# A two-layer recurrent block: layer-1 norm sums kept chunk by chunk in fp32, squared ReLU on ScalarE, the gate through tanh, and the Wq and Wk loads spread out

## The reference, cut to what matters

```
x: (8, 2048, 1024) fp32, one batch element for each core
# layer 0
xn = layernorm(x)
z = sigmoid(xn Wz^T + bz);  h~ = xn Wh^T + bh
s = scan over time of h_t = (1 - z + 1e-8) h_(t-1) + z h~
g = silu( (silu(xn Wg^T) * (xn Wu^T)) Wd^T )      # 3072 hidden, int weights / 127
x = x + s * g
# layer 1
xn = layernorm(x)
s = softmax((xn Wq^T / 32)(xn Wk^T)^T)(xn Wv^T)
xp = xn one token earlier (0 at the first)
xr = mu_r xn + (1 - mu_r) xp;   xk = mu_k xn + (1 - mu_k) xp
k = square(relu(xk W_k^T))
g = silu( sigmoid(xr W_r^T) * (k W_v^T) )
x = x + s * g
```

## Time and profile before

| | us |
|---|---|
| median of three runs | 1475.0 |
| lowest and highest | 1265.99, 1498.23 |
| profiled execution, device time | 1265.23 |
| its span (slowest core, 4) | 1264.2 |
| spans of the eight cores | 1260.6 to 1264.2 |
| TensorE busy | 1191.4 (94%) |
| VectorE busy | 592.3 (47%) |
| ScalarE busy | 299.5 (24%) |
| TensorE idle before its matmuls of L147 | 33.6 |

### The profile page before, as it was taken

The page is one execution under the profiler, slowest core; times in us unless marked ns, Lnnn a source line. Parts: engine busy times, 40 slices in busy tenths (PEclk is TensorE's granted clock), DMA queues, the critical chain, the costliest instruction groups (busy, mean ns, idle before and its releaser), DMA issues.

```text
span 1264.2 us, 16472 instructions; the slowest of 8 cores (1260.6 to 1264.2 us)
## 1 busy us (share of the span) xinstructions
PE 1191.4 (94%) x5728; PEld 547.4 (43%) x5728; DVE 592.3 (47%) x833; ACT 299.5 (24%) x398; POOL 123.4 (10%) x220
## 2 busy tenths in 40 slices
PE   1899999999999999999999786999999999999988
PEld 1344444444444444444444332444444444444443
DVE  3344121444446377144446488233134456556555
ACT  2333211233234211123234412333110101101110
POOL 1011111110111111111104012110000000000000
PEclk9899999999999999999999898999999999999999
DMA  9754844545454485355529647452000012123233
GB/s 202 200 89 85 194 81 71 100 101 112 100 106 67 67 195 93 65 115 104 110 54 151 116 84 131 86 101 83 1 1 1 1 43 80 52 78 83 84 84 117
DMA packets 56963, 116.52 MB, mean 92 GB/s; under 512 B 6704, under 2 KB 14896, under 8 KB 56880
## 3 DMA queue, kind: packets, MB, share of 16 engines
q0 software_dynamic: 31104, 65.03, 31.5%
q1 hardware_dynamic: 25776, 50.43, 12.9%
HBM read 159.47 MB, written 20.97 MB: 143 GB/s over the span
## 4 chain that ended last, share of the span: by engine, by line
PE 87%; DVE 8%; ACT 2%; issue 2%; DMA 1%; DVEq 0%; SPq 0%; ACTq 0%
PE PS L147 85%; DVE S L151 3%; PE PS L712 1%; DVE S L467 1%; DMA S<-xtok 1%; DVE S L426 1%; DVE S L465 1%; PE PS L259 1%; DVE S L463 1%; DVE S L246 1%; ACT S L265 0%; DVEq L62 0%; DVE CB L696 0%; ACT S L395 0%; ACT S L554 0%
## 5 line engine op out<-in xcount | busy, mean ns | idle before, releaser
L147 PE MATMUL PS<-S 128*128 128x512 bf16 x5248 | 1156.1, 383 | 33.6 <-DVE S L151 13.9
L147 PEld LDWEIGHTS PS<-S 128*128 128x128 bf16 x5248 | 514.6, 99 | 659.8 <-issue 61.1
L151 DVE TENSOR_TENSOR S<-S,PS 128x512 bf16<-128x512 bf16 (+1 forms) x128 | 88.0, 688 | 236.2 <-PE PS L147 171.8
L151 DVE TENSOR_TENSOR S<-S 128x512 f32<-128x512 f32 (+4 forms) x124 | 98.6, 795 | 46.7 <-ACT S L554 31.5
L299 ACT ACTIVATE S<-PS 128x512 bf16<-128x512 f32 x96 | 57.3, 597 | 223.7 <-PE PS L147 217.0
L700 ACT ACTIVATE S<-PS,CB 128x2048 bf16<-128x2048 f32 x16 | 31.5, 1967 | 247.9 <-DVE CB L698 247.9
L351 DVE TENSOR_SCALAR S<-S 128x512 f32<-128x512 f32 x32 | 13.7, 427 | 146.7 <-ACT S L346 146.7
L696 DVE TENSOR_REDUCE CB<-PS 128x1 f32<-128x1024 f32 x32 | 39.2, 1225 | 49.2 <-PE PS L739 31.0
L124 POOL DMA_DIRECT2D S<-wg x48 | 27.1, 565 | 307.0 <-PE PS L147 281.0
L638 DVE CAST S<-PS 128x512 bf16<-128x512 f32 x32 | 22.1, 691 | 55.4 <-PE PS L147 55.1
L151 DVE TENSOR_TENSOR S<-PS,S 128x512 f32<-128x512 f32 x32 | 22.1, 691 | 45.5 <-PE PS L147 45.5
(11 more groups left out here) (63 smaller groups left out, 484.1 us busy)
## 6 DMA issues: line engine op xcount, KB each, us to landing
S<-wg POOLq DMA_DIRECT2D x48, 256.0 KB, 4.1
S<-wu POOLq DMA_DIRECT2D x48, 256.0 KB, 4.7
S<-wd POOLq DMA_DIRECT2D x16, 768.0 KB, 7.4
S<-xtok SPq DMA_DIRECT2D x16, 512.0 KB, 17.9
S<-xt SPq DMA_DIRECT2D x16, 512.0 KB, 16.5
x1s<-S SPq DMA_DIRECT2D x16, 512.0 KB, 2.6
S<-x1s SPq DMA_DIRECT2D x32, 256.0 KB, 3.7
out<-S SPq DMA_DIRECT2D x32, 256.0 KB, 2.4
```

Source lines behind the costliest of these rows:

```text
L147: ins = te.matmul(dst, l, r, start=(i == 0), stop=(i == n - 1))
L151: return DVE.did(ve.tensor_mul(o, a, b))
```

## The change

Four things are changed.

- **Norm sums.** While `down_mix` runs chunk e, the new `stat_chunk(h, e - 1)` squares the previous chunk on ScalarE and adds it and its square to two fp32 accumulators on VectorE. After chunk 6 the two accumulators are split into a high and a low bf16 part. `ln1_steps` casts and squares only chunk 7, and sums over the partitions with 3 + 3 matmuls for each span instead of 8 + 8. It now has 17 steps: empty, `cast`, `sums` (both spans), `stat` (both spans), four `affine`, `edge`, eight with two `mix`.
- **Squared ReLU.** ReLU and Square both run on ScalarE, through an fp32 tile; VectorE has no part in it.
- **Gate.** Sigmoid becomes tanh of half the argument, VectorE computes (tanh + 1) * V in one instruction, and ScalarE writes silu of half of that straight into the output tile. That is one VectorE instruction less for each span.
- **Loads.** After each k-stage chunk o of half 0, one Wq piece and one Wk piece are issued, behind that chunk's weight load.

```diff
+        def stat_chunk(h, e):
+            accx, accq, sq = fp(ACCX, 1024), fp(ACCQ, 1024), fp(SQ, 1024)
+            xe = fp(X1 + e * 2048, 1024)
+            ACT.after(x1_tok[h, e], sq_free[0])
+            if e == 0:
+                DVE.after()
+                ACT.after((DVE.sem, DVE.sem.n))
+                acc_tok[h] = ACT.did(se.activation(accq, xe, AF.Square))
+                return
+            t = ACT.did(se.activation(sq, xe, AF.Square))
+            DVE.after()
+            DVE.did(ve.tensor_add(accx, fp(X1, 1024) if e == 1 else accx, xe))
+            DVE.after(t, acc_tok[h])
+            sq_free[0] = acc_tok[h] = DVE.did(ve.tensor_add(accq, accq, sq))
+            if e < 6:
+                return
+            for i, a in enumerate((accx, accq)):
+                DVE.after(mix_free[0])
+                t = DVE.did(ve.tensor_copy(bf(HILO[2 * i], 1024), a))
+                DVE.after(t)
+                acc_tok[h] = DVE.did(ve.tensor_sub(bf(HILO[2 * i + 1], 1024), a, bf(HILO[2 * i], 1024)))
 # down_mix, between the gate's silu and the z and h~ products
+            if e:
+                stat_chunk(h, e - 1)
 # ln1_steps
+            def cast():
+                xe = fp(X1 + 7 * 2048, 1024)
+                DVE.after(x1_tok[h, 7], acc_tok[h])
+                st["xb"] = DVE.did(ve.tensor_copy(xb, xe))
+                ACT.after(x1_tok[h, 7], sq_free[0])
+                st["sq"] = ACT.did(se.activation(sq, xe, AF.Square))
+            def sums():
+                for s in range(2):
+                    ...
+                    PE.after(acc_tok[h], st["xb"])
+                    st["mx", s] = (b, mms(ps(b), [(ones[:], r) for r in (hl[0], hl[1], xb[:, c])]))
+                    PE.after(st["sq"])
+                    st["mq", s] = (b, mms(ps(b), [(ones[:], r) for r in (hl[2], hl[3], sq[:, c])]))
+            steps = [lambda: None, cast, sums, stat]
+            for s in range(2):
+                for q in range(2):
+                    steps.append(lambda q=q, s=s: affine(q, s))
 # before the k stage
-        for c in range(NC8):
-            dma(POOL, bf(WQ + c * 1024, 1024), wqn[c], f_sem)
-            fold_tok = dma(POOL, bf(WK + c * 1024, 1024), wkn[c], f_sem)
 # k stage
-                    ACT.after(mm, rk_free[s], *t_free)
+                    ACT.after(mm, rk_free[s])
                     at = ACT.did(se.activation(rt, ps(b), AF.Relu))
                     bank_free[b] = at
-                    DVE.after(at)
-                    rk_free[s] = kact_tok[s] = mul(bf(KACT + o * 1024 + s * 512, 512), rt, rt)
+                    ACT.after(at)
+                    rk_free[s] = kact_tok[s] = ACT.did(se.activation(dst, rt, AF.Square))
                 w_done(k, mm)
                 if h == 0:
+                    dma(POOL, bf(WQ + o * 1024, 1024), wqn[o], f_sem)
+                    fold_tok = dma(POOL, bf(WK + o * 1024, 1024), wkn[o], f_sem)
                     step(late1)
 # gate stage
-                    ACT.after(mm, r_free[s], *rk_free)
-                    rtok.append(ACT.did(se.activation(bf(RS + s * 512, 512), ps(b), AF.Sigmoid)))
+                    ACT.after(mm, r_free[s])
+                    rtok.append(ACT.did(se.activation(fp(RS + s * 1024, 512), ps(b), AF.Tanh, scale=0.5)))
-                    t = mul(tv, bf(RS + s * 512, 512), ps(bk[s]))
+                    t = DVE.did(ve.scalar_tensor_tensor(tv, fp(RS + s * 1024, 512), 1.0, ps(bk[s]), ALU.add, ALU.mult))
-                    at = ACT.did(se.activation(sg, tv, AF.Sigmoid))
-                    DVE.after(at, go_tok[gq])
-                    t_free[s] = mul(gv, tv, sg)
+                    ACT.after(tt[s], go_tok[gq])
+                    t_free[s] = ACT.did(se.activation(gv, fp(TS + s * 1024, 512), AF.Silu, scale=0.5))
```

More of the change, by code:

```diff
@@ L33 @@
 ST = ZZ + 10240
-MD = ST + 2048
-COLS = MD + 1024
+SQ = ST + 2048
+COLS = SQ + 2048
 KACT, WQ, WK = HB, HB + 8192, HB + 16384
@@ L41 @@
 GG = HS + 2048
+MD, ACCX, ACCQ = ST, HS, ST
 AQK = ZZ
@@ L118, in sems @@
         return [sem(f"{name}{i}") for i in range(n)]
+    DGB = DG[:, 0:8]
     PE, DVE, ACT = Line(te, sem("s_pe")), Line(ve, sem("s_dve"), True), Line(se, sem("s_act"), True)
@@ L321, in x_load @@
             x_tok[h, e] = dma(SYN, fp(X1 + e * 2048, 1024), xt[e * 128:(e + 1) * 128, h * HT:(h + 1) * HT], x1_sem[e])
+        acc_tok = {}
+        sq_free = [None]
+        HILO = [TMP + i * 1024 for i in range(4)]
+        def stat_chunk(h, e):
[19 more added lines that the diff above has]
+                acc_tok[h] = DVE.did(ve.tensor_sub(bf(HILO[2 * i + 1], 1024), a, bf(HILO[2 * i], 1024)))
         def down_mix(h, e, kd, k):
@@ L375, in down_mix @@
             return mm
-        mub, rstd = fp(ST, 512), fp(ST + 1024, 512)
         xn1_tok = {}
@@ L383, in ln1_steps @@
             XR, XK = XRH[h], XKH[h]
-            steps = []
             st = {}
[L386 to L400, removed]
-                    PE.after(st["sq"])
[L402 to L408, removed]
@@ new lines, in ln1_steps @@
+            xb, sq = bf(SQ, 1024), bf(SQ + 1024, 1024)
+            stats = [(fp(ST, 512), fp(ST + 1024, 512)), (fp(SQ, 512), fp(SQ + 1024, 512))]
+            def cast():
[6 more added lines that the diff above has]
+                for s in range(2):
+                    c = slice(s * 512, (s + 1) * 512)
+                    hl = [bf(o, 1024)[:, c] for o in HILO]
+                    PE.after(acc_tok[h], st["xb"])
+                    b = bank()
+                    st["mx", s] = (b, mms(ps(b), [(ones[:], r) for r in (hl[0], hl[1], xb[:, c])]))
+                    PE.after(st["sq"])
+                    b = bank()
+                    st["mq", s] = (b, mms(ps(b), [(ones[:], r) for r in (hl[2], hl[3], sq[:, c])]))
@@ L409, in stat @@
+            def stat():
+                tok = [None, None]
+                for s in range(2):
+                    mub, rstd = stats[s]
+                    (bx, mx), (bq, mq) = st["mx", s], st["mq", s]
+                    DVE.after(mx, st["mq", 1][1])
+                    t = DVE.did(ve.tensor_scalar(mub, ps(bx), 1.0 / D, None, ALU.mult))
+                    bank_free[bx] = t
                     DVE.after(t)
                     t = mul(rstd, mub, mub)
-                    DVE.after(t, st["mq"])
@@ L412, in stat @@
[L412 to L430, removed]
@@ L432, in ln1_steps @@
-                steps += [cast, lambda: None, sums, stat, lambda: affine(0), lambda: affine(1)]
-                steps[-2] = lambda affine=affine: affine(0)
-                steps[-1] = lambda affine=affine: affine(1)
+                    DVE.after(t, mq)
+                    tok[s] = DVE.did(ve.scalar_tensor_tensor(rstd, ps(bq), 1.0 / D, rstd, ALU.mult, ALU.subtract))
+                    bank_free[bq] = tok[s]
+                for f, kw in ((AF.Ln, dict(bias=CB[:, EPS:EPS + 1])), (AF.Exp, dict(scale=-0.5))):
+                    for s in range(2):
+                        ACT.after(tok[s])
+                        tok[s] = ACT.did(se.activation(stats[s][1], stats[s][1], f, **kw))
@@ new lines, in stat, with affine @@
+                st["rstd"] = tok
+            def affine(q, s):
+                mub, rstd = stats[s]
+                xq = chunks(fp(X1 + q * 8192, 4096), 4)[:, :, s * 512:(s + 1) * 512]
+                tq = chunks(fp(TMP + q * 4096, 2048), 4)
+                mb = bass.broadcast_tensor_aps(xq, mub.rearrange("p (c j) -> p c j", c=1))[1]
+                rb = bass.broadcast_tensor_aps(xq, rstd.rearrange("p (c j) -> p c j", c=1))[1]
+                dst = chunks(bf(XN + h * 8192 + q * 4096, 4096), 4)[:, :, s * 512:(s + 1) * 512]
+                DVE.after(st["mq", 1][1])
+                t = DVE.did(ve.tensor_sub(tq, xq, mb))
+                DVE.after(t, st["rstd"][s], xn_ready)
+                xn1_tok[h, s] = mul(dst, tq, rb)
@@ L448, in edge @@
                     pv = chunks(bf(XN, 8192), 8)[:, :, 1023:1024]
-                    df = chunks(bf(MD + 1016, 8), 8)
+                    df = chunks(DGB, 8)
                     t = DVE.did(ve.tensor_sub(df, xf, pv))
@@ L461, in mix @@
                 df = S[:, MD:MD + hi - lo]
-                DVE.after(xn1_tok[h, part], st.get("md"))
+                DVE.after(xn1_tok[h, 1], st.get("md"))
                 t = DVE.did(ve.tensor_sub(df, x, p))
@@ L519, in build_program @@
             late1 = ln1_steps(h, pe_tok)
+            hs_free = collections.deque([acc_tok[h]] * 4)
             l0_tok = pe_tok
@@ L524, in build_program @@
         wvt_sem = sem("s_wvt")
-        kt_slot = collections.deque(range(2))
-        RS, TS, SG, GO = GG, HS, GG + 1024, ZZ
+        RS, TS, GO = GG, HS, ZZ
         r_free = [None] * 2
@@ L532, in build_program @@
         kact_tok = {}
-        rk_free = [None, None]
-        sg_free = None
+        rk_free = [acc_tok[1]] * 2
         ng = 0
@@ L583, in build_program @@
                 for s in range(2):
-                    tv = fp(HS + s * 1024, 512)
-                    DVE.after(rtok[s], vm[s], t_free[s])
```

(4 more changed lines are left out.)

6 lines of the change are left out of this document (2 added, 4 removed).

## The result

The changed kernel took 1228.4 us (four runs, 1228.3 to 1228.5), against 1264.9 to 1266.0 for the runs of the kernel before that belong with its profiled execution. The ratio is 0.9711, with a 95% interval of 0.9694 to 0.9728: 36.8 us less. (The higher times of the kernel before are executions in which the cores of a die ran at a lower clock; they are left out of every ratio here.) The forecast was 1222, 6 us too low, and inside its own range.

A forecast was written before the change was run, and what follows sets the result against it. Bound: TensorE's waits in layer 1 of half 0, behind VectorE's queue, ScalarE and late loads. That layer falls from 213 to 174.5 us, saving 38.5, plus 4.3 in layer 0: 1265.23 becomes 1222 us, range 1213 to 1238.

The forecast's parts named there:

- What bounds the kernel: Outside start-up, TensorE's idle time lies in one stage: layer 1 of half 0, where half 1's norm is stepped through.
- Norm sums, TensorE in layer 0: Half 0's 20 fewer sum matmuls, from a stretch TensorE fills, save 20 x 0.216 = 4.3 us.
- The prediction's own sign of being wrong: Wrong if TensorE waits in layer 0, or VectorE's last `mix` in half 0's gate stage ends after TensorE's last product there.
- the ring: k stage: banks (eight tiles, 13.8 us) cover ScalarE's and VectorE's lateness, but not at the stage's end.
- The k stage: ScalarE ends 3.3 us behind TensorE; V of span 1 waits 1.8 us for the last square in place of 10.84.
- Gate stage: Layer 1, half 0: VectorE's V passes free banks late for chunks 5 and 6, 2.5 us; half 1's k-stage wait goes.
- Tables: Gate stage: no table loads taken for tanh and silu; even alternating, 5.2 us a chunk stays under 6.91.
- Loads: First `wv` landing at 702.9 was a second hold on V's start; spread, loads cost nothing, by 2 to 3 us.
- Clock: Lower granted clock after one of the two waits in layer 1 of half 0: 1.7 us.
- The stage of before: Layer 1 in the kernel before: 213 us, from 662 to 875; afterwards 174.5.
- Rivals: VectorE keeps gate stage 1236 (0.15); late V or tables 1233 to 1236 (0.09); slow transfers 1252, no gain 1255 (0.09 together).
- the chain in `down_mix`: Layer 0: in-order square, addition and z passes hold TensorE; 5 us a chunk gives 1302 us; chance 0.05.

The follow-up runs named there:

- merged step: Changed kernel with sums and stat of the norm in one step, an empty step behind; 1228.3 and 1228.4 us.

## Why the prediction was right or wrong

- **What bounds the kernel.** Right. One stage held the waits, and 34.4 of the 36.9 us came from it.
- **Norm sums, TensorE in layer 0.** The step that failed: 4.3 us forecast with nothing against it, 2.0 measured. The prediction's own sign of being wrong, a wait of TensorE in layer 0, came in. The matmuls went, but the new `sums` takes four banks of eight in one step and `stat` releases them one step later, so TensorE, one hidden chunk of four banks on, finds the ring full: 1.88 us. (The other 0.3 had been lost ahead of the first sums.) I counted the instructions of the step and not the banks that it holds, though the prediction names the ring in the k stage. There VectorE is free and the banks come back in time; in layer 0 its list had the next hidden chunk's products first. The merged step shows it.
- **The k stage.** The mechanism was right, and the chain of ScalarE's work came out as laid down: 2.25 us for 1.8. The bound by VectorE's queue is shown with 14.3 us. The rule of the Trainium skill by which such work belongs on VectorE (ScalarE: Activation LUTs, Rules for kernel authors) fails in this place: with the square on VectorE the kernel takes 1245.3 us in place of 1228.4. The rule compares the two engines' speed for an element; here the queue that the square joins decides, with 14.3 us of wait for it and 2.6 for the cast behind it.
- **Gate stage.** Right in kind, small in size: 2.5 us forecast, 0.87 + 3.10 measured. VectorE's V passes ended 1.3 to 2.0 us later than laid down, counted from the k stage's start (662.0 there; 670.22 - 48 x 0.216 = 659.9 here). The first waited 1.51 us for tanh, which had a table load of 1.28 in front. My "no loads" forgot the one load behind Ln and Exp. No run takes that load away, so its share is not shown. The rounds before were read as 11.5 us; the two between 747.66 and 771.02 are 23.36, 11.7 each.
- **Tables.** Right. One load for 32 pairs of tanh and silu. The estimate by the figures of the Trainium skill (ScalarE: Activation LUTs, What ACT_TABLE_LOAD costs), 7.8 us a chunk, would have needed two changes of table in every chunk.
- **Loads.** Right that the queue was a second hold (11.7 us without the spreading). The bound of 10 us for a landing was too low (14.4), with no wait from it.
- **Clock.** Right, 1.7 us in the sum: the granted clock was 0.69 and 0.81 in the 7 us behind the 3.10 us wait, 0.31 x 3 + 0.19 x 4 = 1.7 us. That it came so close is partly luck, as a wait of 3.11 us had left no mark before.
- **The stage of before, misread.** I took 875 us as its end, the edge of a stretch. The last activation on R starts at 873.1. That made the saving 1.8 us too large. With 2.3 in layer 0 and 2.1 of waits (2.25 + 0.87 + 3.10 + 0.22 for 4.3) these are 6.2 us; the forecast was 6.0 too low, as the stretch behind gave back 0.5. (The start of half 1's k stage was forecast for 748, without the 1.7 us of clock; the last tanh before it starts at 754.1.)
- **Rivals.** None came in at its size. The one on the slower side, the chain in `down_mix`, shows no wait in layer 0 besides the sum banks.

## What to carry to other kernels

Before pricing the removal of a wait, look for the second thing that ends at the same time: two changes that give nothing each may give 7 us together. A side job moved as steps between tiles needs its banks counted, not only its instructions: how many it holds, and in whose list the release stands. Where one engine is late in bursts, spread its side work evenly before making it smaller.

## What the runs showed of the hardware

TensorE's clock after a wait isn't a function of the wait's length alone. With sums and statistics in one step, a wait of 2.76 us was followed by 160 matmuls in 34.69 us on core 1 and in 36.38 on core 7 of one execution. Longer waits did go with more of it. In the changed kernel that wait was 2.03 to 2.25 us, and the matmuls took 34.5 to 34.7 us on all eight cores. With the merged step it was 2.76 to 3.14 us, and they took 35.8 to 36.4 on seven of eight. With R ahead of V, the eight last products took 29.16 us on core 1 and 33.56 on core 6 behind the same wait of 1.32 us; the granted clock of the stretch was 0.94 and 0.82. As the slowest of eight cores counts, a gain of 2 us in one place can vanish in such a draw. What else decides it, these runs don't show.

Tanh and silu alternate on ScalarE behind one table load: 32 pairs, one load of 1.28 us in the changed kernel.
